# AdaLN, gated delta rule and sparse FFN on one core: solutions by a residual step in place of a Newton step on the inverse

## The reference, cut to what matters

```python
h = _layernorm(x) * (1 + ca) + sa
x = x + ga * attn(h)                       # attn: the part below
h = _layernorm(x) * (1 + cb) + sb
x = x + gb * ffn(h)                        # silu(gate) * up, 2 of 4 kept, down

# attn, x (8, 256, 256), 16 key heads of 128, 2 value heads each, 4-tap convolution
q, k = l2norm(conv(x W_q)), l2norm(conv(x W_k));  v = conv(x W_v)
def step(S, inp):                          # over 256 tokens
    q_t, k_t, v_t, b_t, d_t = inp
    Sk = einsum('bhi,bhipj->bhpj', k_t, S)
    dv = b_t[..., None] * (v_t - Sk)
    S = S * d_t + einsum('bhi,bhpj->bhipj', k_t, dv)
    o = einsum('bhi,bhipj->bhpj', q_t, S)
out = out * rsqrt(mean(out*out) + eps) * norm_w * silu(z);  y = out @ W_out
```

## Time and profile before

| what | us |
|---|---|
| median of 3 runs | 1999.02 |
| lowest and highest run | 1995.98, 1999.43 |
| span of the profiled execution | 1992.6 |
| one iteration of the loop in it (1002.58 to 1030.10) | 27.52 |

### The profile page before, as it was taken

How to read it: one execution, slowest core, us unless ns; L and a number is a source line. 1 busy time by engine, 2 the same in 40 slices (tenths; PEclk the granted TensorE clock), 3 DMA queues, 4 the chain that set the end, 5 groups by cost and what they waited for, 6 DMA issues and landing times.

```text
span 1992.6 us, 63706 instructions
## 1 busy us (share of the span) xinstructions
PE 1944.7 (98%) x24518; PEld 1655.2 (83%) x24518; DVE 1788.5 (90%) x2907; ACT 1743.4 (87%) x3591; POOL 1374.6 (69%) x957
## 2 busy tenths in 40 slices
PE   7799999999999999999999999999999999998999
PEld 6478888888888888888888888888888888886888
DVE  7789999999999999999999999999999999997987
ACT  7599999999999999999999999999999999997332
POOL 5467777777777777777777777777777777665552
PEclk9799999999999999999999999999999999999999
DMA  3000000000000000000000000000000000002100
GB/s 118 13 24 2 3 24 3 24 2 24 3 24 3 24 3 3 24 3 24 2 24 3 24 3 24 3 3 24 3 24 3 24 3 2 24 7 86 49 17 22
DMA packets 18013, 36.02 MB, mean 18 GB/s; under 512 B 5804, under 2 KB 14508, under 8 KB 15412
## 3 DMA queue, kind: packets, MB, share of 16 engines
q1 hardware_dynamic: 17716, 31.95, 4.7%
HBM read 29.30 MB, written 2.64 MB: 16 GB/s over the span
## 4 chain that ended last, share of the span: by engine, by line
PE 93%; DVE 3%; issue 1%; ACT 1%; POOL 1%; DMA 0%; POOLq 0%; SPq 0%; ACTq 0%; DVEq 0%
PE bank L668 82%; PE bank L671 10%; DVE cc L1877 0%; DVE tt L1752 0%; DVE b_le L1742 0%; DMA o<-in_x 0%; ACT inv L1448 0%; DVE yl L1945 0%; POOL go L556 0%; DVE cols L1836 0%; DVE ae L1916 0%; DVE maskT L1777 0%; POOL a L565 0%; ACT invT L1453 0%; POOL invT L572 0%
## 5 line engine op out<-in xcount | busy, mean ns | idle before, releaser
L1877 DVE SCALAR_TENSOR_TENSOR cc<-bank,wc,cc 128x510 f32<-128x510 f32 (+2 forms) x768 | 558.9, 740 | 11.3 <-ACT cc L1363 1.5
L668 PE MATMUL bank<-h,w 128*128 128x512 f16 (+1 forms) x1920 | 423.3, 361 | 1.2 <-DVE zg L1990 1.1
L668 PEld LDWEIGHTS bank<-h,w 128*128 128x128 f16 x1920 | 174.8, 98 | 137.1 <-issue 6.6
L1448 ACT ACTIVATE inv<-bank 128x512 f16<-128x512 f32 x384 | 244.9, 638 | 16.0 <-PE bank L668 16.0
L500 POOL TENSOR_TENSOR rn<-n2m,mhalf 128x4 f32<-128x4 f32 x64 | 64.5, 1008 | 274.4 <-DVE n2m L1890 274.4
L1453 ACT ACTIVATE invT<-bank 128x512 f16<-128x512 f32 x384 | 246.9, 643 | 2.0 <-PE bank L668 2.0
L1945 DVE TENSOR_TENSOR yl<-bank,mask 128x512 f16<-128x512 f32 x320 | 219.1, 685 | 6.7 <-PE bank L668 6.6
L668 PE MATMUL bank<-inv,a 128*128 128x64 f16 (+1 forms) x3584 | 218.1, 197 | 3.7 <-ACT inv L1448 3.4
L1363 ACT ACTIVATE cc<-bank,wc 128x512 f32<-128x512 f32 x256 | 178.0, 696 | 31.3 <-PE bank L668 31.3
L668 PEld LDWEIGHTS bank<-inv,a 128*128 128x128 f16 x3584 | 180.8, 98 | 16.1 <-ACT inv L1448 4.6
L668 PE MATMUL bank<-w,h 128*128 128x256 f16 x1536 | 190.0, 274 | 0.0
(11 more groups left out here) (235 smaller groups left out, 5486.6 us busy)
## 6 DMA issues: line engine op xcount, KB each, us to landing
w_raw<-in_wh SPq DMA_DIRECT2D x15, 1032.0 KB, 4.9
out<-sol SPq DMA_DIRECT2D x16, 128.0 KB, 1.7
v<-in_x SPq DMA_DIRECT2D x3, 512.0 KB, 3.8
moving<-rank_store SPq DMA_DIRECT2D x64, 8.0 KB
standing<-rank_store SPq DMA_DIRECT2D x64, 8.0 KB
w_raw<-in_wgate SPq DMA_DIRECT2D x1, 1024.0 KB, 4.9
cc<-in_wup SPq DMA_DIRECT2D x1, 1024.0 KB, 5.0
pt<-gate_store SPq DMA_DIRECT2D x2, 512.0 KB, 4.4
```

Source lines behind the costliest of these rows:

```text
L668: return mm(o_, l_, r_, start=start, stop=stop, skip_group_check=True)
L1448: A(lefts(inv[:, ring(s)], l), halves(bL[0], l), ACT.Copy).then_inc(sig("x_ready"), 1)
L1877: V.scalar_tensor_tensor(dst, src, wc[:, par(s), i, 3 - j:4 - j], dst, ALU.mult, ALU.add).then_inc(sig(f"conv{i}"), 1)
```

## The change

- The Newton step goes: `residue`, `correction`, `refine`, `refined`, the tiles `hm`, `tt` and `twoI`, and with it the last left half (`level_left(5)` and its copy), since only `invT` is used from now on.
- For each chunk c the solution is made in two halves. `base_values(c)`: `invT` times the right side in half precision (`v16` or `rr16`, which POOL casts: `values_half`, `rest_half`). ACT's `base_kept(c)` copies the result to `ub` in half precision. `base_residue(c)`: (`a1` + `a_lo`) times `ub`. DVE's `base_rest(c)`: the right side in float32 minus that, to `rd` in half precision. `corrected(c)` (in `first_values` and `second_values`): `ident16` times `ub` plus `invT` times `rd`, summed in the bank.
- The calls are put in another order on PE, ACT, DVE and POOL. `z_rows(1)` moves to the next iteration, and so do `z_tanh(1)` (ACT) and the `high_half` of `a`. `gate_output` on POOL moves up from `s3` to `s2`.

```diff
-            def residue(s):
-            def refine(s):
+            def base_values(c, s):
+                need(pe, "xt_ready", n * NL + NL)
+                        ins = m(bS[c][:, c_:c_ + P], invT[:, ring(s), g * 4 + c * PV + p_], (v16, rr16)[c][:, c_:c_ + P])
+            def base_residue(c, s):
+                        m(bS[1 - c][:, c_:c_ + P], a1[:, ring(s), u], ub[c][:, c_:c_ + P], stop=False)
+                        ins = m(bS[1 - c][:, c_:c_ + P], a_lo[:, ring(s), u], ub[c][:, c_:c_ + P], start=False)
+            def corrected(c, s):
+                m(bS[c][:], ident16[:], ub[c], stop=False)
+                        ins = m(bS[c][:, c_:c_ + P], invT[:, ring(s), g * 4 + c * PV + p_], rd[c][:, c_:c_ + P], start=False)
...
-            def refined(s):
-                    A(tt[:, 4 * h:4 * h + 4], grid(bS[h]), ACT.Copy).then_inc(sig("tt"), 1)
+            def base_kept(c, s):
+                A(ub[c], bS[c][:], ACT.Copy).then_inc(sig("ub"), 1)
...
-            def correction(s):
-                    V.tensor_tensor(hm[:, 4 * h:4 * h + 4], twoI[:].unsqueeze(1).broadcast_to([P, 4, P]), grid(bS[h]),
-                                    ALU.subtract).then_inc(sig("hm"), 1)
+            def base_rest(c, s):
+                V.tensor_tensor(rd[c].rearrange("p (g n) -> p g n", g=BG), of, bS[1 - c][:].rearrange("p (g n) -> p g n", g=BG),
+                                ALU.subtract).then_inc(sig("rd"), 1)
...
+            def values_half(s):
+                gp.tensor_copy(v16.rearrange("p (g n) -> p g n", g=BG),
+                               v[:, ring(s)].rearrange("p (g c) v d -> p g c (v d)", c=CH)[:, :, 0, :]).then_inc(sig("v16"), 1)
+            def rest_half(s):
+                gp.tensor_copy(rr16, rr).then_inc(sig("rr16"), 1)
...
-                    level_left(5, s1)
-                    bank_z(1, s0, s3)
-                    z_rows(1, s1)
-                    residue(s1)
                     level_right(5, s1)
```

More of the change, by code:

```diff
@@ L41 @@
 RANK = 4
-CONSTS = 18
+CONSTS = 16
 W_SCALE = 64.0
@@ L173, in adaln_deltanet_ffn @@
         blockrows = yl[:, :, 0, :]
-        same = hm
+        same = solv[:, 0:2].rearrange("p i n -> p (i n)").rearrange("p (l s) -> p l s", s=P)
         log_part = sol[:, 3].rearrange("p (t h) -> p t h", h=NV)
@@ L623, in body @@
                 if s0:
+                    queries_low(s0)
+                if s2:
+                    rest_half(s2)
+                if s0:
                     split_weights(s0)
+                if s1:
+                    low_half(s1)
+                if s0:
+                    masked_beta(s0)
+                if s1:
+                    values_half(s1)
+                if s0:
                     key_norm(s0)
-                    masked_beta(s0)
                     decay_beta(s0)
-                if s1 and not s0:
-                    low_half(s1)
+                if s1 and (not s0):
                     for j in range(TL):
@@ L909, in level_right @@
                 ins.then_inc(sig("right_ps"), 1)
-            def residue(s):
[L913 to L923, removed]
-            def refine(s):
+            def base_values(c, s):
                 n = N(s)
                 need(pe, "xt_ready", n * NL + NL)
[L928 to L938, removed]
+                if c == 0:
+                    need(pe, "v16", n + 1)
+                    need(pe, "oo", n)
+                else:
+                    need(pe, "rr16", n + 1)
                 for g in range(BG):
@@ L1051, in body @@
                     return first_body(s0)
+                if s2:
+                    base_values(0, s2)
+                    bank_z(1, s2)
+                    z_rows(1, s2)
+                    base_residue(0, s2)
                 if s0:
@@ L1057, in body @@
                 if s2:
-                    refine(s2)
-                if s1:
-                    key_cross(s1)
-                    level_rows(0, s1)
+                    first_values(s2)
                 if s0:
@@ L1245, in last_bodies @@
                     query_state(s2)
+                    base_values(1, s2)
+                    base_residue(1, s2)
+                    up(0)
                     second_values(s2)
-                    up(0)
                 bank_turn_output(1, s0, s3)
@@ L2225, in body @@
                     z_gate(0, s1)
-                    correction(s1)
+                if s0:
+                    decayed_queries(s0)
+                if s1:
+                    base_rest(0, s1)
                     z_gate(1, s1)
@@ L2246, in last_bodies @@
                     up_weights_low(3)
+                    base_rest(1, s2)
                     hidden_product(0)
```

359 lines of the change are left out of this document (190 added, 169 removed).

## The result

| | before | after |
|---|---|---|
| median of 4 runs each, us | 1997.5 (1995.0 to 1999.43) | 1953.62 (1953.12 to 1954.4) |
| ratio, 95% interval | | 0.9779 (0.9765 to 0.9793) |
| span of the profiled execution, us | 1992.6 | 1952.0 |
| PE / DVE / ACT / POOL busy, us | | 1892.3 / 1794.6 / 1724.4 / 1444.3 |

The change is 2.2% faster. 1936 was forecast, with a range of 1902 to 1975. The measured time is inside, 17.6 us above the forecast. It lies in the forecast's own case (1917 to 1955), 1.4 us short of the case of ACT's queue.

A forecast was written before the change was run, and what follows sets the result against it. PE's queue was taken as the bound: 27.52 - 1.22 - 0.4 + 0.6 = 26.5 us an iteration, 65 us less over 64. With 2 us behind the loop and 6.4 from span to median: 1936 us, range 1902 to 1975.

The forecast's parts named there:

- ACT's queue: Rival: ACT's idle 1.60 us stays as waits, so ACT sets a period of 27.0 us; 1955 to 1993 us, chance 0.22.
- PE's terms: Matmul groups in PE's loop: 3.45 us removed and 2.23 us added, 1.22 us less an iteration.
- New waits: PE's waits in the loop for the longer solution chain: 0.6 us an iteration, bounds 0.15 and 1.75.
- A: PE, `base_values(1)` to `base_residue(1)`: ACT's copy ready at 1.25 us against 1.12 of cover, short by 0.1.
- B: PE, `base_residue(1)` to `second_values`: cover 0.92 us, needed 0.85, up to 0.65 more if DVE is busy; taken as 0.1.
- C: PE, `second_values` to `second_output`: cover 0.7 us, short by 0.15 at best, 0.35 or 0.85 with ACT behind; taken as 0.4.
- Old holes: Small holes hidden in PE's records of the loop before, said to leave with the old order: 0.4 us an iteration.
- The period before: Length of one loop iteration before the change, read from a single window: 27.52 us, PE working 27.48 of it.
- Head and tail: Outside the loop: two more handovers per chunk behind it at about 0.85 us each, less two `tt` copies, +2 us.
- PE full: Rival: no new waits on PE, period 25.9 to 26.2 us, time 1898 to 1917 us, chance 0.16.
- Slower: Rival: waits in the loop exceed 1.62 us an iteration, at 2.15 the period is 28.05 and the time 2035 us; chance 0.09.
- POOL's casts: Two new casts of 512 columns on POOL: 0.55 to 1.16 us each, taken as 1.16, within 7.5 us of idle time.

The follow-up runs named there:

- e10: Changed kernel with each `a_lo` product of the base residues added twice (8 more PE matmuls an iteration): 1967.56 us, ratio 0.985 to the kernel before.
- e4: Changed kernel without the `a_lo` products in both residues (8 fewer PE matmuls an iteration): 1953.39 us, ratio 0.9779 to the kernel before.
- e5: Changed kernel with one convolution tap on DVE computed for 32 of 256 tokens: 1951.38 us, ratio 0.9769 to the kernel before.
- e11: Changed kernel with 288 more elements copied on ACT ahead of the identity's odd columns: 1963.8 us, ratio 0.9829 to the kernel before.
- e7: Changed kernel's products with all four engines' calls in the old order, new calls squeezed in near the old solves: 2245.6 us, ratio 1.125.
- e8: e7 with PE's `second_values` and `second_output` and DVE's `base_rest(1)` issued earlier: 2112.68 us, ratio 1.0577 to the kernel before.
- e2: Changed kernel with DVE's guard of the query norms issued one iteration later, where POOL is idle: 1952.91 us, ratio 0.9784.
- e1: Changed kernel with POOL's `gate_output` ahead of the two `hidden_low` calls in the loop's last iteration: 1951.61 us, ratio 0.9779.

## Why the prediction was right, and what was off

- **What bounds the kernel.** PE's queue was taken as the bound, with ACT 1.6 us away. Right in part: e10's first 0.22 shows PE on the loop, but e4 shows that taking PE's work away gives nothing any more. By the change PE's saving came off one for one, but for 0.65 of holes; behind it nothing more does, as DVE is late in the first chunk and ACT in the second. ACT is idle for 1.0, below the 1.2 forecast.
- **PE's terms.** The sum was -1.22. `base_residue` takes 0.45 for 8 matmuls (1004.29 to 1004.74), 0.056 each as taken. Right.
- **New waits.** Forecast 0.6, measured about 0.65; nothing was taken for the first chunk, and there is none. Spread otherwise than said: A is 0.05 and B 0.15, near the 0.1 each that I had, but C is 0.07 and not 0.4, and two groups between B and C are held for 0.15 each by DVE, by its level copy and its turned output. The reason given for C, ACT behind with `second_kept`, is right all the same. Where DVE is early (e5), C is 0.21, and the stretch is as long as before. So ACT sets the sum of the waits behind the residue. To have met its size by adding up three places is luck in part.
- **Old holes.** 27.34 - 1.22 + 0.65 = 26.77, and 26.46 was measured: so 0.31 went with the old order, where I let 0.4 go. That is a remainder of the sum, not measured by itself.
- **The period before.** This is the term that was mis-sized. I took one iteration as 27.52, and the mean of 59 is 27.34. By the starts of `refine` three of four iterations before take 27.29 and the fourth 27.47, in three cases 27.51 to 27.55. I had read one of these three, with a DMA share of 0.13, where the three behind it have 0.01. After, every one takes 26.46 to within 0.01, but for two (26.58 and 26.63). The target of 26.5 was met (26.46) by luck in part: 0.18 too much at the start was made up for by 0.09 too much for the old holes and 0.05 too little for the new ones. But an iteration gives 0.88 and not 1.02, and 64 of them 56 and not 65.
- **Head and tail.** I had +2. The head gives +2.8 (known to some 2), which I did not consider. Behind the loop it is +8.2. There, in PE's timeline after:

```profile
1774.58 0.23 PE L686 MATMUL bank<-solv,a 128*128 128x128 f16 x1 [1.56 <-ACT solv L1500]
...
1778.54 0.61 PE L686 MATMUL bank<-solv,ident 128*128 128x512 f16 x1 [3.34 <-DVE solv L1984]
```

  and DVE's wait for POOL:

```profile
1777.20 0.69 DVE L2020 SCALAR_TENSOR_TENSOR zg<-zth,bank 128x512 f32<-128x512 f32 x1 [6.62 <-POOL osq L528]
```

  "Two more handovers per chunk at about 0.85 each" was too cheap: with nothing to cover them they are 1.5 to 3.3 (the second chunk's first one, at 1792.24, is 2.09). And the granted clock fell there, which was not in the sum (below).
- **Around the span.** I added 6.4 us; the execution with the span of 1952.0 took 1953.7, so 1.7 us, and in every other execution for which both are known it is 1.7 to 1.9. So the 1992.6 belong to a quicker execution than the median, most likely of about 1994.3 (an estimate by that 1.7).
- **Rivals.** *PE full* missed (26.2 at most). *ACT's queue* has 26.8 to 27.4 as its period, and missed; but its mechanism is there, in the second chunk in every kernel of this order, and ahead of `base_values(0)` in e11. The sign that the forecast named for it, more waiting for the levels' copies than for the new chain, did not show it: 0.27 of the 0.65 is at A, B and C and 0.15 at a level's copy. *Slower* lacks its 1.62 us of waits; e7 and e8 show that it is what happens when the order does not fit.
- **POOL's casts** take 0.61 each, near the lower bound of 0.55, and not 1.16.

The error of 17.6 us as a sum: loop, head and tail give 40.6 of span where I had 63. That is 22.4 too little saved: some 9 by the size of an iteration's gain, some 7 in the first rounds, which gain nothing and take 2.8 more, and some 6 behind the loop. 4.7 too much was put around the span. 22.4 - 4.7 = 17.7.

## What to carry to other kernels

When three in-order queues are all within a microsecond of the period, what one of them loses shows only if the next handover comes earlier too: follow the freed time row by row to the group where it is gone, as in e4, and shorten that one with it. A stretch that keeps its length while two of the three queues get shorter or longer in it, as the second chunk does here, is held by the third. Take the period of a loop from many iterations (first and last row of one marker), not from one; and price the place behind the loop by its own, since there every handover is open. To find whether an engine named by the chain of waits is on the loop, give it more work in front of its wait.

## What the hardware showed that I had not expected

- A DVE instruction on 128 x 4 elements takes 0.88 us while a POOL product of 2.37 us runs, and 0.16 where POOL is idle (e2).
- PE's clock behind the loop. In the windows of after, the granted clock is 0.74 where PE works 12.1 of 20 us, and 0.91 in the next, after 1.00 in the loop. Before, in the windows of that place (1790 to 1870), with PE at work for 16.0 to 16.8 us of 20, it is 1.00 throughout, and also where it works 14.80:

```profile
1770.00:1790.00 20.00, 12.13 (x97) 9.17 (x95) 8.18 (x12) 11.36 (x28) 10.58 (x10) 0.74 0.01 3
1790.00:1810.00 20.00, 16.56 (x139) 13.85 (x137) 13.72 (x17) 9.83 (x18) 5.83 (x5) 0.91 0.32 105
```

  0.74 of the 2.4 GHz level as a mean is some of the stretch at 1.2 GHz. 24 matmuls of 256 columns take 4.79 us here (1782.08) and 2.78 before. In e1, where DVE's wait for POOL is out of the way, the same window has 0.87, and the same 24 (from 1778.64) take 4.04. How the tail's 8.2 us divides between the waits and the clock is open.
